# The low halves of x in the attention are subtracted by GpSimd instead of VectorE, four per batch item, under a semaphore of their own

## What is computed

```
q = query @ Wq + bq;  k = key @ Wk + bk;  v = values @ Wv + bv        # query = x, key = values = context
scores = einsum('bhqd,bhkd->bhqk', q, k) / sqrt(32), NEG_INF where not j < i
attn = softmax(scores);  attn[:, :, 0, :] = 0
x = layer_norm(query + einsum('bhqk,bhkd->bhqd', attn, v) @ Wo + bo)
out = layer_norm(x + relu(x @ W1 + b1) @ W2 + b2)
```

## Time and profile before

| | us |
|---|---|
| median of 3 runs | 2662.8 (2660.74 to 2662.99) |
| the profiled execution, its own time | 2661.86 |
| its span from first to last instruction | 2660.0 |
| attention alone in its regular stretch | about 60 to 1090 |
| handover to the second part | about 1090 to 1260 |
| second part alone | about 1260 to 2660 |

### The profile page before, as it was taken

One profiled execution on the slowest core, in us unless ns is written; L12 is line 12 of the kernel. 1 busy time (PEld: TensorE's weight loads), 2 busy tenths in 40 slices (PEclk: granted clock), 3 DMA queues, 4 the chain that ended last, 5 costly groups with the idle time before them and its releaser, 6 DMA issues.

```text
span 2660.0 us, 62128 instructions
## 1 busy us (share of the span) xinstructions
PE 2596.9 (98%) x22540; PEld 2237.7 (84%) x22540; DVE 2077.8 (78%) x5171; ACT 1525.6 (57%) x2945; POOL 1556.8 (59%) x1721
## 2 busy tenths in 40 slices
PE   7999999999999999878999999999999999999998
PEld 5888888888888888757888888888888888888887
DVE  6889888988888888788767767676767676767675
ACT  4777787787777877677343434343434344444433
POOL 3777777766666666566555545454555544454543
PEclk9999999999999999978999999999999999999999
DMA  7666655565555655556132222222222222222220
GB/s 194 156 154 157 162 152 155 153 151 149 146 141 147 152 140 141 138 135 176 42 70 50 69 52 67 54 64 57 57 64 57 64 57 64 56 65 56 64 57 25
DMA packets 439556, 273.35 MB, mean 103 GB/s; under 512 B 299648, under 2 KB 334400, under 8 KB 439248
## 3 DMA queue, kind: packets, MB, share of 16 engines
q1 hardware_dynamic: 438288, 267.79, 40.4%
q10 hardware_dynamic: 960, 1.57, 0.3%
HBM read 109.86 MB, written 57.67 MB: 63 GB/s over the span
## 4 chain that ended last, share of the span: by engine, by line
PE 92%; DVE 3%; SPq 1%; issue 1%; DMA 1%; POOL 1%; ACT 1%; ACTq 0%; DVEq 0%; POOLq 0%
PE h_ps L1369 25%; PE acc L1385 22%; PE lin_ps L708 13%; PE front L1355 6%; PE lin_ps L704 6%; PE max_ps L683 6%; PE st_ps L730 6%; PE o_ps L750 4%; PE o_ps L752 3%; PE st_ps L765 2%; POOL prob_lo L429 1%; DVE W L1276 1%; SPq L847 0%; ACTq L492 0%; SPq L354 0%
## 5 line engine op out<-in xcount | busy, mean ns | idle before, releaser
L429 POOL TENSOR_TENSOR prob_lo<-probs,prob_hi 128x512 f16<-128x512 f32 (+1 forms) x768 | 784.4, 1035 | 371.7 <-ACT prob_hi L508 366.9
L1369 PE MATMUL h_ps<-x_halves,W 128*128 128x256 f16 x6144 | 756.4, 273 | 2.0 <-ACT hf L1183 2.0
L1385 PE MATMUL acc<-W,hs 128*128 128x256 f16 x5376 | 669.6, 273 | 1.0 <-DVE hs L1329 1.0
L1369 PEld LDWEIGHTS h_ps<-x_halves,W 128*128 128x128 f16 x6144 | 596.5, 98 | 87.8 <-issue 16.8
L1183 ACT ACTIVATE hf<-h_ps,b1s,scale_evac 128x256 f32<-128x256 f32 x512 | 284.8, 562 | 583.5 <-PE h_ps L1369 581.6
L664 DVE CUSTOM_DVE_ANT_0 max_ps<-max_ps,mask_q 128x128 f32<-128x128 f32 (+3 forms) x1024 | 485.5, 505 | 129.3 <-PE max_ps L683 113.2
L1385 PEld LDWEIGHTS acc<-W,hs 128*128 128x128 f16 x5376 | 525.9, 98 | 62.2 <-issue 1.5
L506 ACT ACTIVATE probs<-st_ps 128x512 f32<-128x512 f32 (+1 forms) x768 | 406.5, 529 | 244.2 <-PE st_ps L765 227.2
L1109 POOL TENSOR_TENSOR hf<-hf 128x256 f32<-128x256 f32 x256 | 237.7, 928 | 500.6 <-ACT hf L1183 500.4
L508 ACT ACTIVATE prob_hi<-st_ps 128x512 f16<-128x512 f32 (+1 forms) x768 | 406.8, 530 | 0.0
L1329 DVE TENSOR_TENSOR hs<-hf,hs 128x896 f16<-128x896 f32 x256 | 279.1, 1109 | 142.9 <-ACT hs L1172 142.9
(11 more groups left out here) (119 smaller groups left out, 3761.9 us busy)
## 6 DMA issues: line engine op xcount, KB each, us to landing
heads<-stage SPq DMA_DIRECT2D x756, 128.0 KB, 2.5
raw<-in_xT SPq DMA_DIRECT2D x64, 256.0 KB, 3.1
o_in<-ctx_rows SPq DMA_DIRECT2D x256, 64.0 KB, 2.5
x_in<-in_x SPq DMA_DIRECT2D x32, 512.0 KB, 4.0
x_rows<-x SPq DMA_DIRECT2D x64, 256.0 KB, 2.1
o_in<-x_rows SPq DMA_DIRECT2D x256, 64.0 KB, 2.4
out<-y SPq DMA_DIRECT2D x32, 512.0 KB, 3.1
raw<-in_cT SPq DMA_DIRECT2D x60, 256.0 KB, 3.9
```

The lines of the kernel that those rows point to most:

```text
L429: pool.tensor_tensor(prob_lo[:, k % 4, 0:w], probs[:, k % PROBS, 0:w], prob_hi[:, k % 4, 0:w], ALU.subtract).then_inc(pl_done, 1)
L1369: last = pe.matmul(h_ps[:, f % 2, 0:T], W1[:, aw, j, f * P:(f + 1) * P], x1_halves[:, item.parity, aa, j, :], start=(j == 0 and m == 0), s ...
L1385: last = pe.matmul(acc_products[:, n, :], hs[:, p % HS, aa, n, :], W2[:, p, aw, n, :], start=(p == 0 and m == 0 and n % 2 == 0), stop=(p = ...
```

## The change

The four subtractions of each item leave DVE's stream and are put into POOL's, with the semaphore `x_lo` in place of `lo_done`. `X_SPLIT` is 33 and `FIRST_X_SPLIT` 37, so they stand at slots 34, 37, 40 and 43 (item 0: 37, 39, 41, 43), each behind the `prob_lo` of that slot, which is the 256-wide one. `lo_done` now counts the context and the first splits alone; PE, SP and POOL's line 445 wait for `x_lo` where the low half of x was meant.

```
-    def x_splits(window, slot, j, behind=0):
+    def x_splits(window, slot, j, behind=0, first_behind=0):
...
-        first = due(window, slot, SLOTS, 1, FIRST_X_SPLIT + 2 * j + behind)
+        first = due(window, slot, SLOTS, 1, FIRST_X_SPLIT + 2 * j + first_behind)
...
     def gpsimd(pool):
...
                     pool.tensor_tensor(prob_lo[:, k % 4, 0:w], probs[:, k % PROBS, 0:w],
                                        prob_hi[:, k % 4, 0:w], ALU.subtract).then_inc(pl_done, 1)
+                for j in range(KT):
+                    for item in x_splits(window, s, j, 1 + j, 0):
+                        wait_for(pool, hi_done, NCHUNK, item, chunk_of("x", j) + 1)
+                        pool.tensor_tensor(acts["x"][:, 1, j, :], raw[:, j, :], acts["x"][:, 0, j, :], ALU.subtract
+                                           ).then_inc(x_lo, 1)
...
-                            wait_for(pool, lo_done, NCHUNK, item, chunk_of("x", KT - 1) + 1)
+                            wait_for(pool, x_lo, KT, item, KT)
...
     def vector(dve):
...
                     for item, _ in after_first(due(window, s, SLOTS, B, CTX_SPLIT + 2 * j + 2)):
-                        split(item, "c", j)
-                    for item in x_splits(window, s, j, 2):
-                        split(item, "x", j)
+                        split(item, j)
...
-                    elif n in (0, UNITS.index(("q", 0))):
-                        wait_for(pe, lo_done, NCHUNK, item, chunk_of("cx"[n > 0], j) + 1)
+                    elif n == 0:
+                        wait_for(pe, lo_done, KT, item, chunk_of("c", j) + 1)
+                    elif (kind, t) == ("q", 0):
+                        if first and j == 0:
+                            pe.wait_ge(lo_done, 4 * KT)
+                        wait_for(pe, x_lo, KT, item, j + 1)
```

## The result

The changed kernel took 2675.62 us in the median of six runs (2672.87 to 2677.64), the kernel before 2662.89: a ratio of 1.0045, 95% interval 1.0032 to 1.0058. It is slower by 12.7 us, where 11.85 were forecast. A second set of runs of the same file gave 1.0043 (1.0030 to 1.0055). The profiled execution has a span of 2675.8 us; with 2677.64 us it was the longest of the six.

A forecast was written before the change was run, and what follows sets the result against it. PE, busy 98% of the span, was taken as the bound. 15 x 0.75 = 11.25 us plus 0.6 for the first item made 11.85, so 2674.7 us from 2662.8; own range 2671 to 2679, 8 in 10: 2665 to 2685.

The forecast's parts named there:

- DVE's relief: Regular attention stretch: DVE loses some 3.7 us of work per item, costed at nothing since PE never waits for it.
- DVE was the hidden bound: Rival: weight loads waiting for row maxima start sooner, worth at most 6.8 us, giving 2656 to 2660; chance 0.03.
- POOL's price: Each moved subtraction takes 1.26 us on POOL, ends 1.16 and 1.5, costing 1.22 us of its queue.
- The first place: Slots 37 to 41: x1 makes slot 38's wide `prob_lo` late, so PE stands still 0.65 us an item.
- a delay of the semaphore: At slot 38's wide `prob_lo`: some such delay would make PE's loss 0.70 us instead of 0.65.
- The spare time: Before PE wants slot 38's wide `prob_lo` in slot 41: 0.57 us, which the added 1.22 us exceed by 0.65.
- The second place: Slot 42: its wide `prob_lo` comes late behind x2, 0 to 0.15 us more an item, taken as 0.1.
- x3: Slot 43: x3 ends near 508.1 us, the `prob_lo` of slot 44 near 509.3, wanted near 509.4, so just hidden.
- The first item: Item 0, chain of the start: the low halves end 0.6 us later, or 0 if POOL goes ahead of line 635.
- DVE starves: Rival: POOL's full queue keeps the ports, PE waits for DVE 1 to 1.9 us; 2681 to 2691 us, chance 0.14.

The follow-up runs named there:

- a shorter x1: Against the changed kernel, GpSimd makes only 256 columns of x1 and VectorE the other 256: 2669.72 us, ratio 1.0019.
- a freed narrow one: Against the changed kernel, VectorE's V subtraction of the first unit moved from slot 38 to slot 37: 2670.38 us, ratio 1.0021.
- x2 alone: Against the changed kernel, GpSimd makes only x2 of items 1 to 15, VectorE the rest: 2665.83 us, ratio 1.0010.
- x0 and x2: Against the changed kernel, VectorE makes x1 and x3 of items 1 to 15 again, GpSimd the rest: 2669.5 us, ratio 1.0018.
- without x1: Against the changed kernel, VectorE makes x1 of items 1 to 15 again, GpSimd the rest: 2674.8 us, ratio 1.0039.
- both cures: Against the changed kernel, x1 in halves on both engines and the first unit's V subtraction in slot 37: 2672.33 us, ratio 1.0032.

## Why the prediction was right, and where it was not

**PE bounds it, and DVE's relief is worth nothing: right.** DVE's work fell by 33 us in 800 and nothing came of it; the weight loads still wait 13 times for the maxima, 5.8 us, against 15 and 6.4 in the same stretch before. The rival by which DVE was the hidden bound is out. Its price was misread: 6.0 us in 800 us, or 11.4 items, is 0.53 us an item and 7.9 in all, not 0.45 and 6.8.

**POOL's price: right.** 1.29 us for 1.26.

**The first place: right in kind, too small by a fifth.** Everything in the chain is found again, the 1.20 us of the held narrow one included, and two experiments took it apart: a shorter x1 and a freed narrow one each took 0.5 us off the loss. The term was 0.65 us and measured 0.79 to 0.81. What it left out is the way from POOL's end to PE's start: 579.21 to 579.35 here, 571.75 to 571.90 with the half, 0.14 to 0.15 us in both. I had named a delay of the semaphore and then set it against DVE coming sooner. The spare time was 0.43 us, not 0.57. That PE's list of waits says 0.65 is chance.

**The second place: nil for 0.1 us.** I gave slot 42 0.1 us, and the intervals of the change show none. The order was not the one that I had followed: line 639 isn't held by POOL there but asks first, and POOL's `prob_lo` of slot 41 takes 1.63 us. That of slot 42 still ends 0.18 us before its reader, which needs 0.14 to 0.15. The 0.2 us with x2 alone and 0.3 with x0 and x2 are another loss, by x3 on DVE; where x3 is on POOL too and PE isn't late (without x1, or with both cures), this place costs nothing.

**x3: the wrong reason for a right number.** I asked only if POOL's next `prob_lo` would be in time, and it was. I didn't follow DVE's queue: line 608 and 610, 0.16 and 0.18 us of work, can be held for a whole subtraction each, and with them `onorm` and PE. In the change the second of them (now line 616) is held, for 1.22 us, without harm; in three other kernels both are held, and PE loses 0.8 us an item. By the traces the change escapes this because POOL is later there (see both cures); that was not tried by itself. The same holding of DVE was my rival "DVE starves", whose place I had put at slot 38 instead.

**The first item: 0.4 at its place for 0.6, and not to be seen in the whole.** With item 0 alone on GpSimd 0.3 us were measured, within an interval from -1.6 to 3.2 us. The last product for x of item 0 seems to start sooner than before, but that execution is ahead by then. DVE and PE of the changed kernel:

```profile
16.40 0.68 DVE L639 TENSOR_TENSOR V<-vf,V 128x512 bf16<-128x512 f32 x1
...
22.46 0.96 PE L716 MATMUL lin_ps<-xT,wq 128*128 128x512 f32 x3 [0.27 <-POOL xT L435]
```

From the start of line 639 to that product it is 6.06 us, and it was 22.77 - 17.14 = 5.63, so the place costs 0.43 us. Later it drowns: PE's slot 40 of item 1 began between 75.3 and 79.5 us in the thirteen profiles, whoever made item 0's low halves.

**The sum.** x1's place was given 15 x 0.65 = 9.75 us and cost 15 x 0.79 = 11.9; slot 42 was given 1.5 and cost nothing; the start was given 0.6, and 0.4 is seen at its place: a term too small and two too large, near the right total, and that they cancel is luck. Executions of one kernel spread by some 5 us. The profiles differ at the start, in the late transfers into `heads`, and in the handover, where intervals of 4.5 us in one execution are 3.0 or 5.3 in another; that leaves about 1 us open in any sum here.

**The ports.** All holds seen are of whole instructions, and who begins first wins, down to 0.1 us. The Trainium skill says so in "SBUF — State Buffer", section "Who interferes with whom": issue order and not the shape decides who blocks. The Trainium skill also lists there `tensor_scalar` among the operations that can take both ports, beside those with two SBUF inputs; line 634 above, with one SBUF input and held for 1.20 us, agrees.

No version found is faster than the kernel before: PE has no idle time in the regular stretch that a relief of DVE could fill.

## What to carry to other kernels

Before moving work to an engine with idle time, write down for each result behind the new work when it is ready and when its reader starts; nearly 30% idle time on POOL held only 0.43 us where it mattered. Do the same for every instruction of the other engine that shares its ports, small ones too, since they wait for whole instructions. If only one of a row of like instructions is moved, look at its neighbours that stay: x1 cost 0.47 us an item more with x2 still on DVE, and x2 cost 0.2 only with x3 still there. And test a cure with the others in place: the loss at x1's place hid one at x3's, and with both cures in place 9.0 us were lost, against 5.5 and 6.2 with one.

## What the runs showed that I had not expected

One of four moved instructions cost more than all four: 18.1 against 12.7 us. An operation of 16 columns on DVE can take 1.20 us instead of 0.16 because GpSimd has begun a subtraction 0.12 us before. And PE can lose 0.26 to 0.3 us at a place without a wait in its own list, since the modelled end of a product (0.19 to 0.21 us for one that is followed after 0.03 to 0.05) covers it; only the starts show it.
